# The attention outputs are turned through 36 columns of the identity instead of 128

## What is computed

```
q = rms(q, qn_w); k = rms(k, kn_w)              # 16 query heads of 8, 4 key heads
scores = einsum('bhqd,bhkd->bhqk', q, k) / sqrt(hd)
attn   = softmax(scores)                         # layer 1: with a causal mask
attn   = einsum('bhqk,bhkd->bhqd', attn, v)
attn   = attn.transpose(0, 2, 1, 3).reshape(B, L, D)
```

## Time and profile before

| | |
|---|---|
| runs | 2280.06 us median of 3, from 2272.35 to 2289.49 |
| profiled execution | 2283.65 us, of which the span (first to last instruction) 2281.9 us |
| mean granted TensorE clock | 0.856 of full |
| first attention, its steady part | about 90 to 485 us of the span |
| second attention | about 1488 to 1880 us |

### The profile page before, as it was taken

One profiled execution on the slowest core, in us unless ns is written; L12 is line 12 of the kernel. 1 busy time (PEld: TensorE's weight loads), 2 busy tenths in 40 slices (PEclk: granted clock), 3 DMA queues, 4 the chain that ended last, 5 costly groups with the idle time before them and its releaser, 6 DMA issues. The chain is left out here.

```text
span 2281.9 us, 32065 instructions
## 1 busy us (share of the span) xinstructions
PE 1823.7 (80%) x10443; PEld 761.7 (33%) x10446; DVE 1552.8 (68%) x1549; ACT 1398.3 (61%) x2920; POOL 676.2 (30%) x369
## 2 busy tenths in 40 slices
PE   6799999976886666766666887379998985999985
PEld 1333333333333333333332343124333333333331
DVE  6788888816999999999995322456555634465463
ACT  2377777757999999999993132225454553443432
POOL 1000000003999999999994001100000000000000
PEclk8799999987978887788787988569898896899996
DMA  4211121004666665666661010242232000000000
GB/s 146 54 25 25 25 40 20 2 10 139 208 203 207 200 200 196 196 200 201 199 202 42 27 47 1 72 74 50 39 48 42 16 1 15 0 0 0 0 5 14
DMA packets 56962, 182.30 MB, mean 80 GB/s; under 512 B 8373, under 2 KB 11728, under 8 KB 55312
## 3 DMA queue, kind: packets, MB, share of 16 engines
q1 hardware_dynamic: 56200, 179.74, 26.9%
q10 hardware_dynamic: 648, 1.04, 0.2%
HBM read 160.56 MB, written 7.21 MB: 74 GB/s over the span
## 5 line engine op out<-in xcount | busy, mean ns | idle before, releaser
L680 DVE TENSOR_REDUCE attn_mx<-banks 128x1 f32<-128x1024 f32 (+7 forms) x512 | 502.4, 990 | 180.7 <-PE banks L485 121.7
L630 ACT ACTIVATE attn_probs<-banks 128x512 f32<-128x512 f32 (+3 forms) x896 | 446.0, 550 | 282.2 <-PE banks L513 181.8
L1753 POOL TENSOR_TENSOR hc<-st,ct 128x1024 f32<-128x1024 f32 x256 | 598.7, 2366 | 46.3 <-DVE st L1711 46.2
L1711 DVE TENSOR_TENSOR_SCAN st<-da,banks 128x1024 f32<-128x1024 f32 x256 | 566.6, 2269 | 19.6 <-DVE banks L1703 13.2
L1676 ACT ACTIVATE ut<-b_turned,x_now 128x128 f32<-128x128 f32 x1280 | 389.8, 388 | 2.9 <-PE banks L1569 1.2
L513 PE MATMUL banks<-attn_qa,attn_ka 99*128 99x512 bf16 (+3 forms) x896 | 274.1, 375 | 21.1 <-DMA attn_qa<-attn_mrow 19.0
L1668 ACT ACTIVATE da<-dt,a_now 128x1024 f32<-128x1024 f32 x256 | 284.2, 1138 | 10.6 <-DVE st L1711 8.9
L1569 PE MATMUL banks<-mats,ut 128*128 128x128 f32 x1280 | 237.8, 328 | 58.4 <-DVE st L1711 38.4
L533 PE MATMUL banks<-attn_probs,attn_vst 128*32 128x256 f32 (+3 forms) x3584 | 273.4, 376 | 4.1 <-ACT attn_osb L621 3.8
L483 PE MATMUL banks<-attn_ka,attn_qa 64*128 64x512 bf16 (+3 forms) x512 | 203.1, 397 | 77.1 <-DMA attn_ku<-attn_ka 55.6
L1592 PE MATMUL banks<-hc,onecol 128*32 128x512 f32 x1024 | 182.8, 795 | 97.8 <-POOL onecol L1744 89.0
(11 more groups left out here) (422 smaller groups left out, 1850.4 us busy)
## 6 DMA issues: line engine op xcount, KB each, us to landing
dt<-dt_rows SPq DMA_DIRECT2D x256, 512.0 KB, 4.5
attn_qa<-q_lin SPq DMA_DIRECT2D x144, 64.0 KB
attn_qu<-attn_qa SPq DMA_DIRECT2D x16, 512.0 KB, 4.2
moe_w<-in_moe_w SPq DMA_DIRECT2D x2, 2048.0 KB, 10.1
attn_ka<-k_lin SPq DMA_DIRECT2D x63, 64.0 KB
mats<-in_mats SPq DMA_DIRECT2D x1, 2844.5 KB, 15.0
attn_ku<-attn_ka SPq DMA_DIRECT2D x8, 256.0 KB, 5.0
q_lin<-qparts SPq DMA_DIRECT2D x6, 256.0 KB
```

The costliest lines, as they stand in the source:

```text
L630: nc.scalar.activation(probs[s % 4][:, jj, c0:BLK], scores_exp[jj][:, c0:BLK], ACT.Exp, scale=scale).then_inc(probs_ready, 1)
L680: nc.vector.reduce_max(mx[:, qt, j:j + 1], scores_max[n % 2][:, 0:w], AX.X)\
L1711: nc.vector.tensor_tensor_scan(st[n % 4][:, :], da[n % 4][:, :], pair[:, :, :].rearrange("p h t -> p (h t)"), 0.0, ALU.mult, ALU.add).then ...
L1753: nc.gpsimd.tensor_tensor(hc[n % 8][:, :], st[n % 4][:, :], ct[:, b * SEQ:(b + 1) * SEQ], ALU.mult)\
```

## The change

In `turn_out`, the moving operand is a view of the identity with columns 0 to 8, 32 to 40, 64 to 72 and 96 to 104, so 4 x 9 = 36 columns, with a step of 32 columns between the runs of nine. Each of the four results takes 36 columns of the bank instead of 128, laid side by side, and `out_norm` reads its view from these 144 columns: the sums with a step of 9 elements instead of 32, the values as eight of every nine. The stationary operand, the number of matmuls and of weight loads, all waits and all other lines stay.

```diff
         out_acc = k.bank[6]
+        OUT_ROWS = 4 * (HD + 1)
+        used_rows = k.m("ident").rearrange("p (j c) -> p j c", j=4)[:, :, 0:HD + 1]
         turned = k.bank[7]
@@ turn_out
                     for t in range(4):
-                        last = nc.tensor.matmul(turned[:, sl(t, TILE)], osb[:, sl(t, TILE)], k.m("ident"),
+                        last = nc.tensor.matmul(turned[:, sl(t, OUT_ROWS)], osb[:, sl(t, TILE)], used_rows,
                                                 start=True, stop=True)
                     last.then_inc(oturned, 1)
@@ out_norm
-                    tv = turned[:, :].rearrange("p (t j c) -> p t j c", t=4, j=4)
+                    tv = turned[:, 0:4 * OUT_ROWS].rearrange("p (t j c) -> p t j c", t=4, j=4)
                     link(nc.vector.reciprocal(rden[:, :, :], tv[:, :, :, 8]), 2 * i + qb + 1, own_norm)
```

## The result

The changed kernel took 2308.95 us (median of four runs, 2307.47 to 2311.01), the kernel before 2282.45 us (median of four, 2272.35 to 2289.49: the three runs of the table above and one more): a ratio of 1.012, 95% interval 1.0079 to 1.0161. It is 26.5 us slower. The profiled execution took 2307.84 us with a span of 2306.1.

What follows compares the result with a forecast made beforehand. TensorE's order was taken to set the pace in both attentions. 26 bursts x 0.12 us + 6 x 0.18 = 4.2 us less, from 2280.06 to 2275.9, given as 2276 us; range 2266 to 2290.

Steps and rivals of the forecast that it cites:

- What bounds the kernel: Both attentions: TensorE sets the pace, with some standstill in the second; the first attention's burst is fully on the path.
- The burst: Eight turn matmuls: weight loads set the step, so 36 columns save 0.12 us at full clock, 0.18 at half.
- The operand with gaps: Strided moving operand of the turns: weight loads hide up to 3.6 times the usual column price; no cost taken.
- VectorE: L704 and L707 after each burst: taken as unchanged, within 0.03 us; 0.1 us either way would be hidden.
- Bounds: Saving over all bursts: from nothing up to 28 us if bursts shrink with their columns; 4.2 taken.
- rival (A): All turn bursts: time goes by columns, 28 us less, 2252 us; chance 0.04.
- Whether the gain is kept: Second attention: shorter turns move the DMA chain forward as a whole, so the wait eats nothing and 4.2 us stand.
- Rival (B), the clock: Second attention: clock rises later after the DMA wait, 1.1 us a unit, at worst 3.5 us more, 2284; chance 0.13.
- The page's rule: TensorE's clock gate follows how busy the array has been, so fewer columns can only delay the rise.
- The range: Whole kernel's median: 2266 to 2290 us, the forecast and its slower rivals with the runs' scatter.

Runs made afterwards that it cites:

- 36 / 128: Kernel before with 36 columns only in the causal first-half turns, 128 in all others: 2309.62 us, ratio 1.0114.
- the filled wait: Kernel before with 12 bf16 matmuls of 512 unread columns ahead of the mid-unit causal DMA wait: 2278.61 us, ratio 1.0012 with all turns at 128 columns.
- width_24: Kernel before with 4 x 24 = 96 moving columns in all turns of both attentions: 2298.16 us, ratio 1.0097.
- first_half_full_rows: Kernel before with 36 columns in causal first-half turns, two 128-column unread bf16 matmuls on all 128 rows behind each of their four: 2303.45 us, ratio 1.0122.
- B alone: Kernel before with 36 columns in first attention and causal second-half turns, 128 in first-half ones: ratio 1.014 with unread matmuls filling the mid-unit DMA wait, 1.0028 without.
- width_16: Kernel before with 4 x 16 = 64 moving columns in all turns of both attentions: 2313.4 us, ratio 1.0157.
- fill_mid_wait_narrow: Changed kernel plus 12 unread 512-column bf16 matmuls ahead of the mid-unit causal DMA wait, against the kernel before: 2358.42 us, ratio 1.0357.
- fill_dma_wait: Kernel before plus 12 unread 512-column bf16 matmuls at the start of each causal unit but the first: 2285.99 us, ratio 0.9998.

## Why the prediction was wrong

Point by point:

- **What bounds the kernel**: right. TensorE's order sets the pace, and the shorter burst of the first attention came off its time, 0.09 us a burst.
- **The burst**: right in its mechanism, the saving a little too large. 0.12 us was forecast at full clock and 0.08 measured (1.04 and 1.08 us), 0.18 and 0.16 at half clock (1.90 and 1.92). The weight load sets the step: bursts of 36, 64, 96 and 128 columns take 1.08, 1.10, 1.13 and 1.16 us.
- **The operand with gaps, VectorE**: right. The packed operand takes 1.08 us as well, L704 and L707 stayed at 0.26 and 0.29 us.
- **Bounds, rival (A)**: the time did not go by columns.
- **Whether the gain is kept**: the argument placed the DMA wait at the start of a unit and exchanged the two turns. The chain through L496 was read in the right order of time, but a price for the clock could not be read per turn that way. Nor did TensorE stand still "for some 3.5 us" at each of the seven waits: four lasted 2.8 to 3.8 us, the others 0.3, 1.1 and 1.8.
- **Rival (B), the clock: this is the step that failed, in its size, its place and its chance.** I took the two rises of before as the whole of what the clock can do, 1.1 us a unit, 3.5 us more than before at the worst. I looked only for a later rise after the existing wait, and named as its sign half clock for longer than 11 us after a restart. What the runs showed is two effects. Turn B, narrow, makes the clock fall where before it never fell: beside it stand diagonal matmuls of 128 to 256 columns, and 0.9 us ahead of it a wait of 0.96 us for VectorE, which the kernel before has too. Turn A, narrow, lies where the clock would rise and keeps it down: lows of 31 to 34 us instead of 7 to 17 (36 / 128), and beside the filled wait 48 instead of 27 with B narrow too. In the changed kernel all six lows begin at turn B, and its causal attention is 25.4 us longer, against 1.3 us gained in the other. The price was to be had in part from the trace of before: a unit that stays at high clock takes 40.9 us (1569.78 to 1610.64), the next, with a low of 14 us, 48.9, of which 3.5 are its longer wait and some 4.5 the clock. A unit of the changed kernel with its 27 us of low and no DMA wait takes 51.0, so that the clock alone costs 10 us in each, where the prediction had 1.1.
- **The page's rule**, that the gate follows how busy the array has been (the Trainium skill, "TensorE: Matmul & The Clock Gate", section "What's actually happening"), was in the text with the right sign. The runs agree in that fewer columns came with a lower clock, but the busy time of the profile doesn't show it: 38.76 and 38.80 of 40 us stand beside clocks of 1.00 and 0.66. So the busy time that the profile counts cannot stand for the activity that the page speaks of.
- The range ended at 2290 because (B) was priced so, as 3.5 us and scatter; the result lies 19 us above it.

**What stays open**: what in turn A and B counts. Fewer fp32 columns is the only change made, and 96, 64 and 36 columns lose 1.0, 1.6 and 1.2%. Yet added bf16 columns, on 64 or 128 rows, and added loads did not give it back, and a shift of 0.2 us at 128 columns seems to cost 0.6% (1.0004 to 1.0112). Whether the number of columns, their being fp32 or the exact spacing decides is not settled. Nor is a turn needed for such a fall: the first unit has no turn B among its diagonal matmuls, and in 2 of the 20 traces (width_24 and first_half_full_rows) a low of 20 us begins there, some 2 us after the same wait of 0.96 us and soon after the clock had first risen. So it may be the stretch that lets the clock fall, and 128 columns in turn B that hold it; a kernel with no turn in this place was not run. Nor is it known why B alone costs 1.4% beside the filled wait and is within noise beside the unfilled one; there its lows partly take the place of those after the wait. For the same reason the 25.4 us are not split between A and B. The length of lows comes from one execution of each kernel, and that one can be the fastest by far (width_16: 2293, the other four 2312 to 2318).

## What to carry to other kernels

Moving columns that a weight load covers are hardly worth taking away: eight fp32 matmuls with 128 x 128 weights went from 1.16 to 1.08 us for 72% fewer columns. Where TensorE's clock already falls in some units, price an edit by a whole unit at either clock (here 41 and 51 us) and not by its own length, and look for stretches of small matmuls beside the edit, where the clock does not fall yet. Try such a trim first where the clock is steady: in the first attention, at 1.00, it cost nothing (0.9969, 0.9931 to 1.0008). And run a kernel whose clock wavers several times before reading one profile of it.

## What the runs showed of the hardware

TensorE ran at 1.2 GHz for 27 us (the changed kernel) and 48 us (fill_mid_wait_narrow) while the profile has it busy without a pause. These lows began within 2.5 us of the start of a burst with few columns; the only pause near, 0.96 us, stands there with 128 columns too, and no low followed it then. A low of 27 us made a unit 10 us longer (51.0 against 40.9). Added work that nobody needs can cost nothing: 18 us of unread matmuls (fill_dma_wait) left the time at 2286 us, since the time at half clock went from 68 to 34 us and the waits for the DMA from 16.5 to 5.5. And a moving operand with gaps of 23 columns after every nine took the same 1.08 us as a packed one.
